# Loading two chunks of x one image earlier, 18 of 32 statistics in one unit, and an earlier copy of the content sum, in a lambda-layer kernel

## The reference

```
g   = group_norm(x, 32 groups)                    # mean, variance over 16 channels x 4096 pixels
h   = relu(bn1(conv1x1(g)))                       # 512 -> 128
q   = bnq(conv1x1(h)); k = softmax(conv1x1(h)); v = bnv(conv1x1(h))   # 64, 16, 32 channels
pos = conv2d(v, emb, 15x15, padding 7)            # 16 maps for each of 32 v channels
cl  = einsum('bkm,bvm->bkv', k, v)                # the content sum, 16 x 32
h   = einsum('bhkn,bkv->bhvn', q, cl) + einsum('bhkn,bkvn->bhvn', q, pos)
out = x + relu(bn3(conv1x1(relu(bn2(h)))) + g)    # 128 -> 512
```

## Time and profile before

| what | us |
|---|---|
| median of 3 runs | 4807.04 (4805.04 to 4808.21) |
| the profiled execution, its own time | 4802.3 |
| its span, first to last instruction | 4800.5 |
| PE busy | 4394.3 (92%) |
| DVE busy | 2802.7 (58%) |
| ACT busy | 2335.2 (49%) |
| mean granted TensorE clock | 0.959 of full speed |

### The profile page before, as it was taken

How to read it: one execution, slowest core, us unless ns; L and a number is a source line. 1 busy time by engine, 2 the same in 40 slices (tenths; PEclk the granted TensorE clock), 3 DMA queues, 4 the chain that set the end, 5 groups by cost and what they waited for, 6 DMA issues and landing times.

```text
span 4800.5 us, 121009 instructions
## 1 busy us (share of the span) xinstructions
PE 4394.3 (92%) x49366; PEld 2693.8 (56%) x49366; DVE 2802.7 (58%) x4631; ACT 2335.2 (49%) x2880; POOL 966.8 (20%) x529
## 2 busy tenths in 40 slices
PE   4899999999999999999999999999999999999997
PEld 2555555655565655566555555555555555555554
DVE  3465655665655655556656556656566555566564
ACT  1454445454445554455544454544555544445444
POOL 0022202122211222112222121222112221112222
PEclk8899999999999999999999999999999999999998
DMA  2688778898878897788887788987888977889876
GB/s 94 212 283 288 245 269 276 277 306 271 261 270 269 283 307 256 257 277 284 282 297 245 265 278 274 304 270 249 280 271 283 306 255 252 271 269 304 267 246 246
DMA packets 537174, 1284.17 MB, mean 268 GB/s; under 512 B 43048, under 2 KB 225324, under 8 KB 528556
## 3 DMA queue, kind: packets, MB, share of 16 engines
q1 hardware_dynamic: 456396, 992.83, 63.8%
q10 hardware_dynamic: 80352, 284.45, 16.8%
HBM read 844.79 MB, written 432.33 MB: 266 GB/s over the span
## 4 chain that ended last, share of the span: by engine, by line
PE 59%; issue 12%; DMA 9%; DVE 6%; SPq 6%; POOL 4%; ACT 3%; ACTq 2%; POOLq 0%; DVEq 0%
PE ring L526 15%; PE ring L652 13%; PE ring L507 12%; PE ring L582 8%; DMA X<-x_dram 4%; DMA q_parts<-region 3%; DVE st L892 3%; PE ring L606 2%; POOL region L1191 2%; PE ring L533 2%; PE ring L616 2%; ACTq L813 2%; PE ring L538 2%; POOL X L1198 1%; SPq L402 1%
## 5 line engine op out<-in xcount | busy, mean ns | idle before, releaser
L701 ACT COPY region<-ring 126x1024 f32<-126x1024 f32 x1120 | 1103.2, 1015 | 971.7 <-PE ring L507 958.1
L582 PE MATMUL ring<-h,w3T 128*128 128x512 f32 x2048 | 991.5, 624 | 22.9 <-ACT h L720 13.2
L526 PE MATMUL ring<-X,w1e 128*128 128x512 f32 x2048 | 909.0, 597 | 3.2 <-DVE w1e L918 3.2
L652 PE MATMUL ring<-region,V 126*32 126x128 f32 x24576 | 874.9, 286 | 34.3 <-issue 34.2
L507 PE MATMUL ring<-Qt,Ep 96*126 96x256 bf16 x5120 | 759.4, 288 | 47.7 <-ACT region L701 30.8
L652 PEld LDWEIGHTS ring<-region,V 126*32 126x32 f32 x24576 | 686.1, 115 | 196.8 <-issue 191.1
L701 DVE COPY region<-ring 126x1024 f32<-126x1024 f32 x416 | 507.0, 1219 | 439.9 <-PE ring L507 416.6
L892 DVE BATCH_NORM_STATS2 st<-X 128x6 f32<-128x512 f32 x1024 | 624.7, 678 | 196.4 <-DMA X<-x_dram 196.3
L507 PEld LDWEIGHTS ring<-Qt,Ep 96*126 96x126 bf16 x5120 | 578.5, 141 | 252.9 <-issue 160.2
L526 PEld LDWEIGHTS ring<-X,w1e 128*128 128x128 f32 x2048 | 385.0, 191 | 469.6 <-issue 466.3
L582 PEld LDWEIGHTS ring<-h,w3T 128*128 128x128 f32 x2048 | 380.0, 198 | 406.1 <-issue 374.1
(11 more groups left out here) (130 smaller groups left out, 3263.4 us busy)
## 6 DMA issues: line engine op xcount, KB each, us to landing
X<-x_dram SPq DMA_DIRECT2D x132, 2048.0 KB, 20.0
out_dram<-X SPq DMA_DIRECT2D x512, 512.0 KB, 7.9
X<-x_dram ACTq DMA_DIRECT2D x124, 2048.0 KB, 10.2
V<-v_windows SPq DMA_DIRECT2D x96, 1024.0 KB, 10.9
Qt<-q_parts SPq DMA_DIRECT2D x582, 128.0 KB, 4.1
lambda_sums<-S SPq DMA_DIRECT2D x64, 1024.0 KB, 4.9
h<-lambda_sums SPq DMA_DIRECT2D x256, 256.0 KB, 5.0
q_parts<-region SPq DMA_DIRECT2D x128, 256.0 KB, 4.2
```

Of the source, the lines that this page charges most:

```text
L526: last = nc.tensor.matmul(dst[:, hh * HALF:(hh + 1) * HALF], w1e[:, c, :], X[:, j, c, hh * HALF:(hh + 1) * HALF], start=(c == 0), stop=(c ...
L582: last = nc.tensor.matmul(dst[:, yb * HALF:(yb + 1) * HALF], w3T[:, t, :], src, start=True, stop=True)
L652: last = nc.tensor.matmul(bank_of(i)[c * DV:(c + 1) * DV, (g % 4) * P:(g % 4 + 1) * P], V[0:TROWS, VSLOT[t], xb, yb * DV:(yb + 1) * DV], W ...
L701: return engine_copy(dst, src)
```

## The change

It has three parts. SP issues the next-but-one image's x chunk 0 behind load_v and chunk 1 between the stores of tiles 11 and 12; chunks 2 and 3 stay at the head of the lambda stretch. The statistics of units 1, 2, 3 are 8, 6, 18 where they were 8, 10, 14. ScalarE's copy of the content sum stands right behind its q loads, ahead of the two relus.

```diff
-STATS_AT = {1: (0, 0, 0, 0, 2, 2, 2, 2), 2: (1, 1, 1, 1, 0, 2, 2, 2), 3: (2, 2, 2, 2, 2, 2, 2, 0)}
+STATS_AT = {1: (0, 0, 0, 0, 2, 2, 2, 2), 2: (1, 1, 1, 1, 0, 2, 0, 0), 3: (3, 3, 2, 2, 2, 2, 2, 2)}
...
             def lam(b, last):
                 if not last:
-                    for j in range(NCH):
+                    for j in range(2, NCH):
                         sp.wait_ge(out_done[j], b * (16 * CT) + HEAD)
                         load_x(b + 1, j)
...
+            def load_ahead(b, j):
+                sp.wait_ge(out_done[j], b * (16 * CT) + 16 * CT + HEAD)
+                load_x(b + 2, j)
+
+            def image(b, ahead):
                 lam(b, False)
...
                 load_v(b + 1)
-                for n in range(7, 16):
+                if ahead:
+                    load_ahead(b, 0)
+                for n in range(7, 12):
                     store_out(b, n)
+                if ahead:
+                    load_ahead(b, 1)
+                for n in range(12, 16):
+                    store_out(b, n)
+
+            sp.wait_ge(c_full, NCH)
+            for j in range(2):
+                load_x(1, j)
+            with nc.Fori(0, B - 2, engines=OrderedEngineSet([sp.engine]), hint_back_edge=True,
+                         head_slot={sp.engine: 0}) as b:
+                image(b, True)
+            image(B - 2, False)
...
-                    elif name == "cl":
-                        keys_out(AT_MIX, b + 1)
...
                     if name == "k3":
                         load_q(b + 1, 2)
+                        keys_out(AT_MIX, b + 1)
```

More of the change, by code:

```diff
@@ L450, in lam @@
                 shuffle(b, 1)
-            with nc.Fori(0, B - 1, engines=OrderedEngineSet([sp.engine]), hint_back_edge=True,
-                         head_slot={sp.engine: 0}) as b:
+            def load_ahead(b, j):
+                sp.wait_ge(out_done[j], b * (16 * CT) + 16 * CT + HEAD)
+                load_x(b + 2, j)
+            def image(b, ahead):
                 lam(b, False)
```

## The result

The changed kernel takes 4841.62 us (median of 8 runs, 4828.81 to 4854.83), against 4806.82 us for the kernel before (8 runs). The ratio is 1.0074, with a 95% interval of 1.0056 to 1.0091: slower by 0.74%, where 1.2% faster was forecast, and above the range. The profiled execution has a span of 4838.8 us and a mean granted clock of 0.948 (before 0.959).

A forecast was written before the change was run, and what follows sets the result against it. PE, busy 92% of the span, was taken as the bound; 1.8 + 1.9 + 1.1 - 1.7 - 0.9 - 0.4 = 1.8 us an image, 56 us over 31 images, gave 4751 us from 4807.0, range 4695 to 4806.

The forecast's parts named there:

- part 2: SP's x chunks 0 and 1 loaded ahead: only these land earlier, chunk 3 lands when it did; no gain booked.
- The 5.7 us a chunk: SP's x loads: time per chunk, from chunk 0's landing at 2510.2 to chunk 3's at 2527.5.
- The margin: DVE in unit 3: chunk 3 first read at 2529.2 against a landing at 2527.4, 1.8 us to spare.
- part 3: Statistics 8/6/18 on DVE: 1.9 us saved at unit 3's content and 1.1 us of slow clock, against waits in unit 3.
- 0.4 us an image for a late chunk 3: DVE in unit 3: loss booked because the 1.8 us margin may be as large as the scatter between images.
- rival C: Chunk 3 late, DVE's statistics and w5.1, w5.3, gm behind it: slower from 3.6 us of lateness, 4850 at 5 us; chance 0.12.
- The 0.9 us I took for it: PE behind the wait at w5.3: loss booked for a possible slow clock, ends 0 to 1.7 us.
- Part 1: Copy of the content sum ahead of two relus: cp 2.2 us earlier, w0.0 then waits 1.3; 1.8 us an image gained.
- The wait at w5.3: PE waits for DVE's slot copies behind the 18 statistics of unit 3: 1.7 us an image lost.
- my terms for it: Statistics table, us an image: 1.9 and 1.1 gained at unit 3's content, 1.7 and 0.9 lost at w5.3.
- A: The clock stays up behind w0.0 and w5.3, chunk 3 in time: 3.8 us an image, 4689 us; chance 0.15.
- B: Gates at w0.0 and w5.3 take nearly all: gain 0, about 4807 us, halfway 4785; chance 0.21.

The follow-up runs named there:

- e10: Copy of the content sum moved and statistics 8/6/18, x loads as before, with load_v3 issued behind the first shuffle; 1.0005 of the kernel before, 4808.3 us.
- e8: The changed kernel with statistics of chunks 2 and 3 taken from chunks 0 and 1 again; 0.9931 of the kernel before, 4769.4 us.
- e9: Copy moved and statistics 8/6/18, x loads as before, with four useless 256 KB stores ahead of chunk 3; 1.0137 of the kernel before, 4867.1 us.
- e1: The kernel before with the copy of the content sum moved alone; 0.9976 of the kernel before, 4784.9 us.
- e2: The kernel before with the statistics table 8/6/18 alone; 0.9918 of the kernel before, 4763.5 us.
- e6: The changed kernel with only chunk 0 loaded ahead, chunk 1 back at the head of the lambda stretch; 1.0024 of the kernel before, 4811.3 us.
- e5: The kernel before with the copy moved and statistics 8/6/18, all x loads where they were; 0.9909 of the kernel before, 4754.4 us.
- e7: The changed kernel with the store of tile 7 put ahead of x chunk 0; 1.0037 of the kernel before, 4818.9 us.

## Why the prediction was wrong, point by point

**The step that failed** is part 2: "It adds no transfer ... chunk 3 lands when it did, since as many bytes stand ahead of it." As many bytes stand there, but they move more slowly in the new order: chunk 3 lands at 119.0 instead of 117.2, chunk 2 at 111.7 instead of 109.7. I had worked out one time for each store and load from a stretch of stores followed by a stretch of loads, and used it for a queue in which they alternate and stand beside V loads. No row of the trace showed that case. The 5.7 us a chunk were a mean as well: chunks take 5.2 us each, and chunk 3 takes 7.5 because of load_v3 behind it (e10), so it matters too what stands behind a chunk, not only the bytes ahead of it.

**The margin** was the second error, in part 3. I had DVE at chunk 3 at 2529.2, 118.4 from the mark, against a landing at 116.6. In the image above DVE was ready at 2546.1, or 118.6, but that agreement is luck: it had waited 0.79 us for chunk 2, and content of that image started late. In the mean DVE is ready at 117.8, and at 116.7 in e8, where it waits for no late chunk, since PE comes to unit 3 at 110.1 and not at the 111.7 (2522.5) of my sum. And chunk 3 landed at 117.2 in the mean before, not at the 116.7 of the one image that I read. So of the 1.8 us nothing was left even had the landing stayed, and 1.8 us of lateness all counted.

**The size of its effect** was the third. I booked 0.4 us an image for a late chunk 3, and in rival C 1 us for each us beyond the margin, with 3.6 us of lateness needed to turn the sign. The mechanism of C, DVE before statistic 24 (28 of 30 images), with w5.1, w5.3 and gm behind it, is what happened, but 1.8 us were enough. In e9, 2.1 us cost 3.3 us an image: the waits come with a slow clock through units 4 and 5. The 0.9 us I took for it stand against 7.4 us more at half clock, which at full work is half of that, 3.7 us. Not all of it is chunk 3's: e8 still has 5.1 us an image at half clock, about PE's own waits with no releaser, which the sum didn't have.

**Part 1** was right in each step (cp's wait 7.7 us for a forecast 10; w0.0 waits 1.5 us for 1.3; no slow clock), and worth 2.1 us at w0.0 and 2.5 at content of unit 0, for a forecast 1.8. It isn't worth that at the end. Alone (e1) it gains 0.24%, 0.4 us an image: the next gate, chunk 0 against w3.5, takes it. In the changed kernel that gate is open (chunk 0 lands at 88.7), the gain reaches unit 3, and there it meets chunks 2 and 3. I looked only one gate ahead.

**Part 3** was mis-sized to the other side. Content's wait and slow clock went, as forecast. The wait at w5.3 that "18 statistics" should cost was forecast at 1.7 us and a slow clock; e2 has 1.1 us of slot waits an image, and e8, with all early chunks, 0.4. What my row for PE left out are its own waits with no releaser: between content of unit 3 and gm they are 0.6 us an image in e2 and 1.7 in e8 (before 0.1). That they cover part of DVE's is likely, but not shown. The table alone gains 0.82%, 39 us, where my terms for it came to 0.4 us an image.

**The rivals.** A's numbers never came up for the changed kernel. B's form, everything given back, is near e6. C was right in kind at 0.12, with too large a threshold; that its 4850 us lie near the measured 4841.6 is chance, since they were for 5 us of lateness. I cited the rule of the Trainium skill's page "DMA: Bandwidth & Descriptors", section "Queues, rings and completion order", on rings in order: e9 agrees (1 MB more ahead of it, chunk 3 2.1 us later). What I drew from it, that only the bytes ahead count, doesn't hold: it says nothing on rate, and it was the rate that changed, and in e10 taking 1 MB from behind chunk 3 made it land 2.9 us earlier.

What stays open: why the rate falls when chunk 0 follows the V loads and about chunk 1, and what makes PE's instructions late.

## What to carry to other kernels

A transfer moved ahead in a full queue gives its own time to what it passes, and the new order can lower the rate for all behind it; ask first which transfer is the last one somebody waits for, and don't touch what is ahead of that one. Treat a margin that is as large as the scatter between images as no margin, since a wait it opens can be followed by a slow clock that costs more than the wait. When a wait is closed, find the next gate behind it before booking the gain, and try the parts of a change alone: here the table by itself (e2), or with the copy (e5), is 0.8 to 0.9% faster than before, and the third part turned that into a loss.

## What the runs showed of the hardware that I had not expected

At the same busy share of the DMA engines (1.03), the same queue moved 394 or 315 GB/s in the mean of 80 to 85 us from the mark, by what stood side by side: V loads with stores behind them, or with a load of x; one store between them brought back 384 (e7).

A transfer issued behind another slowed it: with load_v3 behind it chunk 3 took 7.5 us, without 5.1 (e10).

The granted clock fell to half in units 4 and 5 in 27 of 30 images of the changed kernel, for up to 13.7 us in a row (a mean clock of 0.77 from 120 to 135 us from the mark, 0.99 before), about idle stretches of 0.7 to 3 us among small matmuls, while the single wait of the earlier trace rows was followed by 3.4 us at half.

PE's waits with no releaser of over 0.3 us, 61 of 61 in the images of before and 70 of 70 of the changed kernel, ended 1.2 to 1.6 us after a 16 KB packet of the instruction queue.
